# A graph layer and a slice-attention layer on one core: the table's last store split in two, and GpSimd writes the first block's one-hots before it waits for the table

## The reference, cut to what matters

```python
n   = layernorm(x)
agg = segment_sum(n[src], dst, 6250)
h   = relu(agg @ W_rel + b_rel + n @ W_root)             # 6250 x 512
i, _, g, o = split(h @ W_ih.T + b_ih + b_hh, 4)
y   = (sigmoid(o) * tanh(sigmoid(i) * tanh(g))) @ W_fc + b_fc
x   = x + y
m   = layernorm(x)
sw  = softmax((heads(m @ W_x + b_x) @ W_slice + b_slice) / clip(temperature))   # 8 heads, 64 slices
tok = weighted sums of heads(m @ W_fx + b_fx) by sw, attention among the 64 slices of a head
out = x + (back from slices to nodes by sw) @ W_out + b_out
```

## Time and profile before

| what | us |
|---|---|
| median of 3 runs (1247.07 to 1253.03) | 1250.91 |
| the profiled execution's own time | 1246.6 |
| its span | 1244.8 |
| TensorE busy | 1113.5 (89%) |
| GpSimd busy | 793.0 (64%), 798 table gathers recorded |
| VectorE busy | 833.0 (67%) |
| ScalarE busy | 627.7 (50%) |

### The profile page before, as it was taken

The page is one execution under the profiler, slowest core; times in us unless marked ns, Lnnn a source line. Parts: engine busy times, 40 slices in busy tenths (PEclk is TensorE's granted clock), DMA queues, the critical chain, the costliest instruction groups (busy, mean ns, idle before and its releaser), DMA issues. The chain is left out here.

```text
span 1244.8 us, 30252 instructions
## 1 busy us (share of the span) xinstructions
PE 1113.5 (89%) x9821; PEld 970.4 (78%) x9821; DVE 833.0 (67%) x2580; ACT 627.7 (50%) x1257; POOL 793.0 (64%) x836
## 2 busy tenths in 40 slices
PE   1056889999999999999999999999999999999998
PEld 0045778788888887888888877888888888897798
DVE  7885466677566856776667666766676667646665
ACT  6862435545454545544554455445645554545332
POOL 5367777777777777777777777777777777400000
PEclk9997899999999999999999999999999999999999
DMA  9574444544554445444544454444444554223498
GB/s 329 205 248 120 123 117 147 150 133 122 150 150 140 128 139 148 139 128 136 150 142 138 126 150 139 141 126 148 140 140 127 148 147 137 90 60 99 129 347 291
DMA packets 92942, 188.74 MB, mean 152 GB/s; under 512 B 20890, under 2 KB 55567, under 8 KB 92797
## 3 DMA queue, kind: packets, MB, share of 16 engines
q0 software_dynamic: 39168, 107.01, 30.4%
q1 hardware_dynamic: 42770, 59.89, 14.8%
q10 hardware_dynamic: 10859, 20.05, 4.5%
HBM read 154.87 MB, written 32.00 MB: 150 GB/s over the span
## 5 line engine op out<-in xcount | busy, mean ns | idle before, releaser
L676 POOL DMA_INDIRECT ring<-table,sidx x798 | 765.3, 959 | 266.0 <-issue 260.3
L414 PE MATMUL ps<-h_h,wih_h 128*128 128x250 f32 x1200 | 338.2, 282 | 0.0
L415 PE MATMUL ps<-h_l,wih_h 128*128 128x250 f32 x1200 | 336.0, 280 | 0.0
L416 PE MATMUL ps<-h_h,wih_l 128*128 128x250 f32 x1200 | 336.0, 280 | 0.0
L414 PEld LDWEIGHTS ps<-h_h,wih_h 128*128 128x128 f32 x1200 | 229.6, 191 | 2.0 <-issue 0.8
L415 PEld LDWEIGHTS ps<-h_l,wih_h 128*128 128x128 f32 x1200 | 229.6, 191 | 1.1
L416 PEld LDWEIGHTS ps<-h_h,wih_l 128*128 128x128 f32 x1200 | 229.5, 191 | 0.0
L820 ACT ACTIVATE gate<-ps,bgate 128x250 f32<-128x250 f32 x300 | 124.4, 468 | 138.3 <-PE ps L416 138.3
L1048 PE MATMUL ps<-ring,oneh 128*32 128x512 f16 x2280 | 147.3, 386 | 46.3 <-DMA ring<-table,sidx 35.5
L1475 DVE TENSOR_SCALAR oneh<-iota,didx 128x64 f16<-128x64 f16 (+2 forms) x1199 | 183.5, 259 | 0.9 <-issue 0.9
L1048 PEld LDWEIGHTS ps<-ring,oneh 128*32 128x32 f16 x2280 | 61.3, 97 | 114.4 <-DMA ring<-table,sidx 48.0
(11 more groups left out here) (212 smaller groups left out, 2499.2 us busy)
## 6 DMA issues: line engine op xcount, KB each, us to landing
sp_ring<-table SPq DMA_DIRECT2D x1920, 1.0 KB
ring<-table,sidx POOLq DMA_INDIRECT x798
swt_d<-swt ACTq DMA_DIRECT2D x25, 500.0 KB
gate<-swt_d SPq DMA_DIRECT2D x19, 500.0 KB, 5.7
x_room<-in_x SPq DMA_DIRECT2D x12, 512.0 KB, 10.5
xn<-table SPq DMA_DIRECT2D x25, 224.0 KB
xin<-in_x SPq DMA_DIRECT2D x25, 224.0 KB
res<-xin SPq DMA_DIRECT2D x25, 224.0 KB
```

Source lines behind the costliest of these rows:

```text
L414: eng.matmul(dst, wh, xh, start=first, stop=False)
L415: eng.matmul(dst, wh, xl, start=False, stop=False)
L416: return eng.matmul(dst, wl, xh, start=False, stop=last)
L676: pool.indirect_dma_start(ring[:, j, :], None, table, bass.IndirectOffsetOnAxis(ap=idx, axis=0)).then_inc(done, 16)
```

## The change

The store of the 106 rows becomes two, of 96 and of 10 rows (both counted on the same semaphore, so the waits on it ask for 16 more). GpSimd loads the flag after the raw gathers and, where it is 0, writes block 0's one-hots with 20 tensor_scalar of its own, then scales sp_idx, then waits for the table. DVE loads the flag before the last ln_low; after the branch it writes block 1's one-hots and then runs slice_weights. The statistics of the even pieces among the raw ones (k = 14, 16, 18) go to PSUM bank SUM_B, no longer to SUM_A, the bank in which block 0's sums are made. Where the flag is 1, everything is in the order of before.

```diff
+    REST_PARTS = ((0, REST // 16 * 16), (REST // 16 * 16, REST))
...
-        ln_mv = ps[:, SUM_A:HB:HA - SUM_A, 0:LR * 2].rearrange("p q (r k) -> p q r k", r=LR)
+        ln_mvs = [ps[:, b, 0:LR * 2].rearrange("p (r k) -> p r k", r=LR) for b in (SUM_A, HA, SUM_B)]
+
+        def ln_mv(k):
+            return ln_mvs[1 if k % 2 else 0 if k <= NCH else 2]
...
             else:
-                eng.dma_start(table[RP * P:N, :], lt[TILES][0:REST, 0, :]).then_inc(ln_out[k % TILES], 16)
+                for u, v in REST_PARTS:
+                    eng.dma_start(table[RP * P + u:RP * P + v, :], lt[TILES][u:v, 0, :]).then_inc(ln_out[k % TILES], 16)
...
+        def hots(eng, b):
+
+            e, (plan, _) = b % 2, hot_plan(b)
+            after(eng, sum_done[e], b // 2)
+            for j, (w0, w1, at) in plan.items():
+                n = WIN * (w1 - w0)
+                last = eng.tensor_scalar(oneh[:, e, at:at + n], iota[:, WIN * w0:WIN * w1], didx[:, j:j + 1],
+                                         -float(WN * b), ALU.subtract, ALU.is_equal)
+            last.then_inc(hot_done[e], 1)
...
             for j in range(RAW):
                 gather_x(j)
-            pool.wait_ge(ld_small, 16 * NSMALL)
-            pool.tensor_scalar(sp_idx[:, :], sp_idx[:, :], float(4 * C), None, ALU.mult).then_inc(spi_done, 1)
             pool.wait_ge(plan_done, 1)
             general = pool.value_load(flag_i[0:1, 0:1], min_val=0, max_val=1)
-            for q in range(TILES):
-                pool.wait_ge(ln_out[q], 16 * len(range(q, NCH + 1, TILES)))
-            pool.sem_inc(go, 1)
+            pool.wait_ge(list_d, 2)
...
             with pool.If(general):
+                scale_rows()
+                table_stored()
...
+            with pool.Else():
+                hots(pool, 0)
+                scale_rows()
+                table_stored()
...
+            general = dve.value_load(flag_i[0:1, 0:1], min_val=0, max_val=1)
             ln_low(dve, NLN - 1)
-            slice_weights()
-            general = dve.value_load(flag_i[0:1, 0:1], min_val=0, max_val=1)
...
-            dve.wait_ge(list_d, 2)
-
-            def hots(b):
...
+            with dve.Else():
+                dve.wait_ge(list_d, 2)
+                hots(dve, 1)
+                slice_weights()
...
             def turn(t, odd, gather, gnn, ffn, ahead):
                 if isinstance(t, int) and t == 0:
-                    hots(0)
-                    hots(1)
                     add_halves(0, 0)
                     low_w1()
-                    hots(2)
+                    hots(dve, 2)
```

More of the change, by code:

```diff
@@ L428, in store_chunk, with out_count @@
             else:
-                eng.dma_start(table[RP * P:N, :], lt[TILES][0:REST, 0, :]).then_inc(ln_out[k % TILES], 16)
+                for u, v in REST_PARTS:
+                    eng.dma_start(table[RP * P + u:RP * P + v, :], lt[TILES][u:v, 0, :]).then_inc(ln_out[k % TILES], 16)
+        def out_count(q):
+            return 16 * (len(range(q, NCH + 1, TILES)) + (len(REST_PARTS) - 1 if q == NCH % TILES else 0))
         @block.sync
@@ L468, in _ @@
             for q in range(TILES):
-                sp.wait_ge(ln_out[q], 16 * len(range(q, NCH + 1, TILES)))
+                sp.wait_ge(ln_out[q], out_count(q))
             sp.dma_start(r4[:, 0:CT, :], a["W_rel"].rearrange("(k p) n -> p k n", p=P)).then_inc(ld_w1, 16)
@@ L666, in _, with scale_rows, table_stored @@
                 gather_x(j)
-            pool.wait_ge(ld_small, 16 * NSMALL)
-            pool.tensor_scalar(sp_idx[:, :], sp_idx[:, :], float(4 * C), None, ALU.mult).then_inc(spi_done, 1)
             pool.wait_ge(plan_done, 1)
             general = pool.value_load(flag_i[0:1, 0:1], min_val=0, max_val=1)
-            for q in range(TILES):
-                pool.wait_ge(ln_out[q], 16 * len(range(q, NCH + 1, TILES)))
-            pool.sem_inc(go, 1)
+            pool.wait_ge(list_d, 2)
+            def scale_rows():
+                pool.wait_ge(ld_small, 16 * NSMALL)
+                pool.tensor_scalar(sp_idx[:, :], sp_idx[:, :], float(4 * C), None, ALU.mult).then_inc(spi_done, 1)
+            def table_stored():
+                for q in range(TILES):
+                    pool.wait_ge(ln_out[q], out_count(q))
             def gather(j, idx, done):
@@ L719, in ln_dev @@
                 act.wait_ge(ln_var, k + 1)
-                act.activation(sd[0:n, k % 2, 0:rows], ln_mv[0:n, k % 2, 0:rows, 1], ACT.Sqrt,
+                act.activation(sd[0:n, k % 2, 0:rows], ln_mv(k)[0:n, 0:rows, 1], ACT.Sqrt,
                                bias=eps[0:n, :]).then_inc(ln_sd, 1)
@@ L997, in _ @@
                 pe.sem_inc(gen_mm, 2)
-                pe.wait_ge(wxs_c, 3)
+                pe.wait_ge(wxs_c, CT + 2)
                 with pe.Fori(0, NG) as g:
@@ L1335, in ln_stats @@
                 for r in range(rows):
-                    last = dve.bn_aggr(ln_mv[0:n, q, r, :], stats[0:n, q, r, :])
+                    last = dve.bn_aggr(ln_mv(k)[0:n, r, :], stats[0:n, q, r, :])
                 last.then_inc(ln_var, 1)
@@ L1343, in ln_scale @@
                 link(dve.reciprocal(rstd[0:n, q, 0:rows], sd[0:n, q, 0:rows]))
-                dve.scalar_tensor_tensor(out=nmr[0:n, q, 0:rows], in0=ln_mv[0:n, q, 0:rows, 0], scalar=-1.0,
+                dve.scalar_tensor_tensor(out=nmr[0:n, q, 0:rows], in0=ln_mv(k)[0:n, 0:rows, 0], scalar=-1.0,
                                          in1=rstd[0:n, q, 0:rows], op0=ALU.mult, op1=ALU.mult).then_inc(ln_rstd, 1)
@@ L1394, in slice_weights @@
                 b3 = biasx[:, :].rearrange("p (h g) -> p h g", g=G)
-                link(dve.tensor_tensor(b3, ps[:, SLICE[CT], :].rearrange("p (h g) -> p h g", g=G),
-                                       bsl.unsqueeze(1).to_broadcast([P, H, G]), ALU.add))
+                dve.tensor_tensor(b3, ps[:, SLICE[CT], :].rearrange("p (h g) -> p h g", g=G),
+                                  bsl.unsqueeze(1).to_broadcast([P, H, G]), ALU.add).then_inc(wxs_c, 1)
+                dve.wait_ge(wxs_c, CT + 1)
                 dve.tensor_tensor(b3, b3, rtemp[:, :].unsqueeze(2).to_broadcast([P, H, G]), ALU.mult).then_inc(wxs_c, 1)
@@ L1465, in _ @@
                 link(dve.tensor_scalar(didx[:, :], didx[:, :], float(4 * NOWHERE), None, ALU.add))
-            dve.wait_ge(list_d, 2)
-            def hots(b):
[L1471 to L1477, removed]
+                hots(dve, 0)
+                hots(dve, 1)
+            with dve.Else():
+                dve.wait_ge(list_d, 2)
+                hots(dve, 1)
+                slice_weights()
             def add_halves(p, e):
@@ L1657, in turn @@
                 if gather and gnn:
-                    hots(2 * t + 1)
+                    hots(dve, 2 * t + 1)
                 if gnn:
@@ L1668, in turn @@
                 if ahead:
-                    hots(2 * t + 2)
+                    hots(dve, 2 * t + 2)
                 if ffn:
```

## The result

The changed kernel took 1241.56 us (median of 4 runs) beside 1251.97 for the kernel before: a ratio of 0.9924, 95% interval 0.9901 to 0.9948. Timed once more on another chip it took 1239.36 (5 runs) beside 1246.96: 0.9937 (0.9923 to 0.9950). By these ratios that is 9.5 and 7.9 us faster (the medians differ by 10.4 and 7.6); 7.5 was forecast, and 1243.4 us.

A forecast was written before the change was run, and what follows sets the result against it. GpSimd's stream of table gathers plus a fixed tail bounds the kernel. Store -2.4, branch -0.3, DVE +0.5 and hole -5.34 make -7.5 us, from the median 1250.9 to 1243.4 us; range 1239.5 to 1250.

The forecast's parts named there:

- The stream of gathers sets the end: Whole kernel: it ends when GpSimd's table gathers let it, plus a fixed tail; the change is worth what moves the stream.
- The store: End of the 106-row table store: in two parts its data lands 2.4 us sooner (bounds 1.5 to 3.0).
- The branch: GpSimd before the first table gather: flag and branch ahead of the table wait gain 0.3 us (0 to 1.1).
- The one-hots: Block 0's twenty one-hots on GpSimd: 0.3 us each, 10 us with three holds, done at about 52.
- the cover: GpSimd's idle time before the table is stored hides the one-hots; it is gone from 0.72 us each.
- The rival of a slow operation: GpSimd's one-hots are slow: past 0.72 us each the stream starts later, slower overall from 1.1 us each; chance 0.12.
- DVE's loss: DVE operations delayed by GpSimd's one-hots before the last store: 0.5 us lost (nothing to 1.6).
- The hole: GpSimd's wait before the sixteenth gather, for block 0's sums: all 5.34 us gained, sums done at 78.9.
- what I had to spare: Block 0's sums done at 78.9, sixteenth gather due at 80.3: 1.4 us to spare.
- The banks: Moving the statistics to another PSUM bank changes no operation.
- Its signs of being wrong: One-hots over 0.7 us each, L632 over 1.3 us, the sixteenth gather waiting for L1048, or later waits for slots.
- the third one: Sign of being wrong on GpSimd: one-hots over 0.7 us each.

The follow-up runs named there:

- the second profile: Another profile of the changed kernel itself, with no further edit: span 1237.6 us.
- e5_table_first: Changed kernel with GpSimd's wait for the table ahead of its twenty one-hots instead of behind them: 1250.20 us, ratio 1.0027 to the kernel before.
- e6_twice: Changed kernel with twenty more such one-hot operations on GpSimd ahead of block 0's, into tiles nothing reads then: 1245.08 us, ratio 0.9987 to the kernel before.
- e10_sp16: e8_both with SyncE fetching 16 chunks row by row instead of 15, so GpSimd gathers one less: 1237.72 us.
- e1_store: Kernel before with only the last store split into 96 and 10 rows: 1246.95 us, ratio 0.9997 to the kernel before.
- e9_one_store: e7_banks with the last store in one, 106 rows: 1239.84 us, ratio 0.9943 to the kernel before.
- e7_banks: Changed kernel with the statistics in the two banks of before and block 0's sums waiting for the last of them: 1237.88 us.
- e8_both: e7_banks with the sixteenth gather also waiting only for the first three rounds of block 0's products: 1237.83 us.
- e11_sp17: e8_both with SyncE fetching 17 chunks row by row instead of 15: 1245.04 us, ratio 0.9980 to the kernel before.

## Why the prediction was right, step by step

- **The stream of gathers sets the end: right.** The last gather starts 8.15 us earlier in the second profile, and the time is 7.9 less. Delays put in by hand came out nearly the same: 11.3 us at the first gather and 11.8 at the sixteenth cost 10.8 (e5_table_first), 6.8 and 6.7 cost 5.7 (e6_twice). What counts is the stream up to the last gather for which TensorE waits, and not its very end: a gather less behind that one gave nothing (e10_sp16). The stretch from the last gather to the end, said to be as long as before, was 170.0 us instead of 169.0, inside what it wanders by.
- **The store: right as a stretch, too high as a term.** 5.32 us became 3.04, 2.3 against 2.4 forecast. But it counts in full only if the sixteenth gather waits for nothing. Alone it gave nothing (e1_store); in the changed kernel, where that gather waits for 0.6, it moved it by 1.4; and where block 0 is in time it moved it by 2.1 and the time by 1.9 (e9_one_store against e7_banks).
- **The branch: right.** From SP's going on to the first gather it is 0.69 us instead of 1.12, 0.43 against 0.3.
- **The one-hots: the size was off, the cover held.** Not 0.3 but 0.38 to 0.60 by the width, and 1.35 to 1.50 for those that met an L641. GpSimd's groups by form of the second profile show one of each, in windows of 0.9 us from 54.4, from 51.5 and from 44.3 (the second number is the mean ns of one):

```profile
L651 POOL TENSOR_SCALAR oneh<-iota,didx 128x32 f16<-128x32 f16 x3 | 1.1, 384 | 0.0
```

```profile
L651 POOL TENSOR_SCALAR oneh<-iota,didx 128x64 f16<-128x64 f16 x2 | 1.0, 492 | 0.0
```

```profile
L651 POOL TENSOR_SCALAR oneh<-iota,didx 128x96 f16<-128x96 f16 x1 | 1.4, 1420 | 0.0
```

The third is a held one; unheld, 96 columns take 600 ns. Five one-hots were held, each by another L641, not three, and the scaling met a sixth (1.55 us, not 0.4). GpSimd was done at 56.9, not 52, 3.8 us ahead of the first gather. The rival of a slow operation had its point at 0.72 us each besides the holds; with e6_twice's doubling the cover is gone, as it has to be.
- **DVE's loss: too high.** 0.5 taken. In the second profile the L641 in which the first one-hot starts has 1.34 us instead of 1.21, and that of the 106 rows, beside the scaling, 0.51 instead of 0.42: 0.2. The store is issued 0.47 us later than before (56.96 and 56.49), but 0.33 of that was there before any one-hot: the raw gather of 36.46 starts at 36.79. The four other L641 that met one-hots kept their 1.21 to 1.23, so the lock of the Trainium skill (SBUF — State Buffer, SBUF: two separate sides), which runs both ways, shows here nearly only against GpSimd.
- **The hole: right by 4.7 of 5.34.** Two things met. The sums ended at 79.32, not 78.9, and the sixteenth gather was due at 79.5, not 80.3, because no gather of the first fifteen was held by an L641 (in the profile of before one was, 1.62 instead of 0.95). That second one is the term I missed: it is 0.7 us of gain by itself, and it used up half of what I had to spare. It is also luck: a gather is held if it starts inside an L641, and nothing in the change sees to it that none does (in e5_table_first one is held again, 1.53 us from 73.36, inside the L641 of 73.11). From the start, the hole and that gather it is 2.24 + 4.74 + 0.71 = 7.69 at the sixteenth, and 80.14 is 7.69 before 87.83. The forecast had 7.5 there; it is this near because the 0.7 nobody had counted on makes up for the 0.6 that stayed of the hole.
- **Given back: 0.4.** Two gathers at 82.65 and 84.12 take 1.17 and 1.09 us instead of 0.95. They start inside the last operation of slice_weights (L1428, 82.31 to 83.00) and inside low_w1 (L1639, from 83.71), which the new order puts there, and the stream is 7.3 ahead at the twenty-first.
- **The banks: nothing, it was said, and block 0 was later by them.** They let TensorE start its sums 0.7 us earlier and end them 1.0 later. What that cost in time isn't shown.
- **Its signs of being wrong.** Two of them came, both small: the sixteenth gather waited for the sums (0.6 us), and one L641 was over 1.3 (1.34). The one-hots' mean, 0.70, is at the third one's bound of 0.7.

## What to carry to other kernels

Where one stream sets the end, ask of each edit ahead of it what the next thing is that the stream waits for: two savings in front of the same wait don't add (the 2.3 us of the store gave 1.9 where the sixteenth gather waited for nothing, and nothing where it waited for block 0). And ask it at the other end too: work taken away behind the last thing that is waited for gives nothing. Work put into a hole is free up to the hole's end, and the engine's price must be taken with what holds it there: a one-hot of 0.38 to 0.60 us alone was 0.70 on average among DVE's operations (14.05 / 20), where 0.3 was forecast. And starting TensorE as soon as possible on work that comes in pieces is not always the sooner end; 0.7 us of waiting first gave 1.0 us back at the end of block 0.

## What the runs showed of the hardware

- GpSimd's tensor_scalar on 32, 64 and 96 columns of float16 with a column of scalars has records of 0.38, 0.49 and 0.60 us where nothing holds it, with next to no overlap (the twenty records add up to 14.37 us in a stretch of 14.05), against 0.15 us from start to start on DVE (44 in 6.64). While a DVE tensor_tensor with two SBUF inputs runs, it all but stands still: the twenty took 14.05 us beside L641 of 1.21 us and 12.44 beside those of 0.94.
- Products of 32 columns, which run four side by side, took 625 ns each where two waits broke up the work ahead of them and 381 to 582 behind 27 in a row, with a clock column of 1.00 for both 625 (changed kernel) and 381 (e8_both). Where the column says 0.50 they take 625 as well (e8_both, 79.5 to 83 us). In stretches this short a product's own duration tells the clock better than the column.
- A store of 106 rows took 5.3 us to be waited for, one of 96 and one of 10 took 3.0.
- SyncE issues a row of 1 KB about every 0.39 us (39 in 15.14, e10_sp16); with 17 chunks of them its loads of x came late, eight times (16.8 us of waiting on DVE, e11_sp17).
